# Rebuilding the stage ahead of the attention loop: block firsts and rows read from the input, counting on ScalarE, 64 degree classes, tables beside the last tiles

## The reference

```
xn  = layernorm(x)
q, k, v = xn @ Wq.T + bq, xn @ Wk.T + bk, xn @ Wv.T + bv      # 8 heads of 32
sim = sum(q[dst] * k[src]) / sqrt(32);  p = softmax over the edges of one dst
x   = x + (sum over edges of p * v[src]) @ Wo.T + bo  +  mix(xn)
x   = x + ffn(layernorm(x))       # 8 experts, top 1, capacity 977 per expert
```

## Time and profile before

| | us |
|---|---|
| median of 3 runs | 2949.57 |
| lowest and highest run | 2949.54, 2952.72 |
| span of the profiled execution, first to last instruction | 2949.1 |
| busy PE, DVE, ACT, POOL in that span | 2127.7, 2429.0, 1010.5, 2119.7 |

### The profile page before, as it was taken

The page is one execution under the profiler, slowest core; times in us unless marked ns, Lnnn a source line. Parts: engine busy times, 40 slices in busy tenths (PEclk is TensorE's granted clock), DMA queues, the critical chain, the costliest instruction groups (busy, mean ns, idle before and its releaser), DMA issues. The chain is left out here.

```text
span 2949.1 us, 36213 instructions
## 1 busy us (share of the span) xinstructions
PE 2127.7 (72%) x9400; PEld 1712.6 (58%) x9401; DVE 2429.0 (82%) x3296; ACT 1010.5 (34%) x4314; POOL 2119.7 (72%) x2220
## 2 busy tenths in 40 slices
PE   5675777767776777767888876556666655599998
PEld 4473555555565666555666554444444435599997
DVE  5676788888888999999999888899999985366665
ACT  3220555556566666611111111011111114345353
POOL 4465777777777777777777777777777775567785
PEclk9796888998999999989999898887888885599999
DMA  6746777777777777788888887777777758423331
GB/s 218 246 156 172 208 210 208 207 211 217 219 218 219 218 219 218 227 233 241 257 255 257 254 241 213 212 211 211 211 211 211 211 162 288 152 70 76 88 92 15
DMA packets 257830, 587.19 MB, mean 199 GB/s; under 512 B 49410, under 2 KB 135505, under 8 KB 257565
## 3 DMA queue, kind: packets, MB, share of 16 engines
q0 software_dynamic: 150480, 467.10, 57.4%
q1 hardware_dynamic: 97947, 109.47, 11.2%
q10 hardware_dynamic: 9296, 9.44, 0.9%
HBM read 519.05 MB, written 71.76 MB: 200 GB/s over the span
## 5 line engine op out<-in xcount | busy, mean ns | idle before, releaser
L1041 POOL DMA_INDIRECT wide<-kv_d,arena x1099 | 1051.0, 956 | 335.0 <-issue 326.7
L1340 PE MATMUL ps<-wide,arena 128*128 128x264 f32 x2432 | 694.6, 448 | 238.9 <-DVE wide L1444 238.6
L1340 PEld LDWEIGHTS ps<-wide,arena 128*128 128x128 f32 x2432 | 530.2, 223 | 395.2 <-DVE wide L1444 283.4
L1041 POOL DMA_INDIRECT arena<-kv_d,arena x539 | 515.3, 956 | 164.3 <-issue 159.1
L1176 ACT ACTIVATE ps<-wide 128x256 f32 x229 | 88.8, 388 | 1324.2 <-DVE arena L1410 1282.5
L1413 DVE TENSOR_REDUCE arena<-arena 128x64 f32<-128x2048 f32 x229 | 523.5, 2286 | 7.9
L1340 PE MATMUL ps<-arena 128*128 128x264 f32 x1216 | 350.4, 451 | 128.7 <-DVE arena L1444 128.7
L1410 DVE TENSOR_TENSOR arena<-wide,ps 128x2048 f32<-128x2048 f32 x153 | 349.3, 2283 | 105.7 <-DMA wide<-kv_d,arena 105.6
L1340 PEld LDWEIGHTS ps<-arena 128*128 128x128 f32 x1216 | 267.0, 225 | 209.0 <-DVE arena L1444 152.9
L1444 DVE TENSOR_TENSOR wide<-wide,ps 128x2112 f32<-128x2112 f32 x152 | 356.8, 2347 | 24.4 <-ACT arena L1191 24.4
L141 PE MATMUL ps<-halves 128*128 128x256 f32 (+2 forms) x2304 | 361.9, 319 | 3.2 <-DVE halves L1703 1.6
(11 more groups left out here) (310 smaller groups left out, 3137.8 us busy)
## 6 DMA issues: line engine op xcount, KB each, us to landing
wide<-kv_d,arena POOLq DMA_INDIRECT x1099, 3.8
arena<-in_w SPq DMA_DIRECT2D x16, 1024.0 KB, 5.4
kv_d<-wide SPq DMA_DIRECT2D x49, 260.0 KB, 2.2
arena<-xn_d SPq DMA_DIRECT2D x82, 128.0 KB, 3.4
arena<-kv_d,arena POOLq DMA_INDIRECT x539, 3.8
hb_d<-arena SPq DMA_DIRECT2D x16, 516.0 KB
q_d<-wide SPq DMA_DIRECT2D x49, 128.0 KB, 2.7
xn_d<-arena SPq DMA_DIRECT2D x7, 896.0 KB, 9.0
```

The source lines that it names most:

```text
L1041: e.indirect_dma_start(out=kvb[k][:, j, :], out_offset=None, in_=kv_d, in_offset=bass.IndirectOffsetOnAxis(ap=ixb[k][:, j:j + 1], axis=0)) ...
L1340: m = e.matmul(psE[(k + 1) % 3][:, 0:264], ident, kvb[b][:, j, 256:ROW], start=(j == 0), stop=(j == J - 1))
```

## The change

- **Firsts and rows from the input.** `dst` is no longer copied to DRAM and padded. SyncE's first three issues read each block's first edge from the input. The block numbers are made ahead of the first tile, as element offsets, capped at the last whole block, and the first three row gathers are issued there. The other 47 keep coming three per tile, each behind a tile's product; each quarter of them has a semaphore of its own.
- **Counting on ScalarE.** The comparison and sum over quarters on VectorE are replaced by 50 activations `Sign` with a sum, one per column, three per tile from tile 6 on; the list `LANDED` says from which tile on a quarter may be counted. `ranks` starts in tile 23 without waiting steps and with two steps per tile.
- **64 classes.** The degree one-hots, sums, prefixes and rank products use 64 classes instead of 128, eight columns per step instead of four, and VectorE multiplies and sums a step in two instructions.
- **Tables beside the last tiles.** `tables` no longer waits for the stores or issues queries; it runs on with the steps of the last tiles, and one of its products moves from `ps[6]` to `ps[4]`.
- **Queries.** The function `first_queries` follows the last tile: SyncE writes the edge numbers into `q_d` there, and GpSimd's 13 query gathers wait for that, for the sort and for the last stores.
- **Weights and biases.** Their order becomes keys, queries, values, so that the bias takes two instructions instead of three. ScalarE scales and rounds the weights in three pieces; group 0 is centred on ScalarE like the others.
- **Blanks.** A blank tile is written to DRAM once, and SyncE fills `hb_d` from it by two transfers in each of the loop's eight `AUX` rounds.

The core of the diff:

```diff
+CLS = 64
...
+LANDED = ((6, 13), (11, 26), (15, 39), (19, 50))
+SORTED_FROM = 23
...
+        t_f0 = v(V.memset(fi_i[:, 12:13], 1 << 20))
+        whole = 12 * 128 * 128
+        dma(Y, fi_i[:, 0:12], dst[0:whole].rearrange("(a p j) -> p a j", p=128, j=128)[:, :, 0], s_fi, allow_slow_non_contiguous=True)
+        wait(Y, t_f0)
+        rest_ = NB - 1 - 12 * 128
+        dma(Y, fi_i[0:rest_, 12:13], dst[whole:whole + rest_ * 128].rearrange("(p j) -> p j", j=128)[:, 0:1], s_fi, allow_slow_non_contiguous=True)
+        t_fi = dma(Y, fi_i[rest_:rest_ + 1, 12:13], dst[(NB - 1) * 128:(NB - 1) * 128 + 1].rearrange("(a j) -> a j", j=1), s_fi)
...
-        dma(Y, flat(dst_d)[0:E].rearrange("(a b) -> a b", b=825), dst.rearrange("(a b) -> a b", b=825), s_ed)
...
-        assert E + 86 == NB * 128
...
-        t_fi = dma(Y, fi_i, dst_d.rearrange("(a p) j -> p a j", p=128)[:, :, 0], s_fi, allow_slow_non_contiguous=True)
+        s_bl = sem("s_bl")
...
+        t_bl = dma(Y, blank_d, blank, s_bl)
 
...
+        t = v(V.tensor_scalar(out=off, in0=blk, scalar1=128.0, scalar2=float(E - 128), op0=ALU.mult, op1=ALU.min))
+        wait(V, t)
+        t_off = v(V.tensor_copy(blki, off))
...
-        def take_rows(t_blk):
-            wait(G, t_blk, t_ed)
-            for c in range(50):
-                s_row.inc(G.indirect_dma_start(out=rows[:, c, :], out_offset=None, in_=dst_d,
-                                               in_offset=bass.IndirectOffsetOnAxis(ap=blki[:, c:c + 1], axis=0)), 16)
...
+        def take_rows():
+            for q, (c0, c1) in enumerate(QUARTERS):
+                for c in range(c0, c1):
+                    s_row[q].inc(G.indirect_dma_start(out=rows[:, c, :], out_offset=None, in_=dst.rearrange("(a b) -> a b", b=825),
+                                                      in_offset=bass.IndirectOffsetOnAxis(ap=blki[:, c:c + 1], axis=1)), 16)
...
-            wait(Y, t_own)
-            ids_of = q_d.rearrange("(p c) d -> p c d", c=NT)
-            dma(Y, ids_of[:, 0:32, 256:QI], own[0].bitcast(f32), s_own)
-            t_own_.append(dma(Y, ids_of[:, 32:NT, 256:QI], own[1].bitcast(f32), s_own))
...
+        fetching.append(take_rows())
+        fetch_some(t_off)
...
+        def count_some(n):
+
+            for _ in range(n):
+                c = counted[0]
+                q = [i for i, (c0, c1) in enumerate(QUARTERS) if c0 <= c < c1][0]
+                wait(S, (s_row[q], s_row[q].n), t_half)
+                counted[1] = a(S.activation(less[:, c, :], rows[:, c, :], ACT.Sign, bias=nodeh[:, c:c + 1], scale=-1.0,
+                                            accum_out=fine[:, c:c + 1]))
+                counted[0] = c + 1
...
         def ranks():
...
-            fetching[0] = take_rows(v(V.tensor_copy(blki, blk)))
-            for _ in range(WAIT_ROWS):
-                yield
-            assert fetching[0] is None
-            wait(V, (s_row, s_row.n))
-            for c0, c1 in QUARTERS:
-                t = v(V.tensor_tensor(less[:, c0:c1, :], rows[:, c0:c1, :],
-                                      nodeid[:, c0:c1].unsqueeze(2).to_broadcast([128, c1 - c0, 128]), ALU.is_lt))
-                yield
...
-                t = v(V.tensor_reduce(fine[:, c0:c1], less[:, c0:c1, :], AX.X, ALU.add))
...
+            wait(V, counted[1])
+            t = v(V.scalar_tensor_tensor(out=rp, in0=fine, scalar=0.5, in1=half, op0=ALU.mult, op1=ALU.add))
...
+                t = v(V.tensor_tensor(OHc[:, c0:c1, :], iota[:, 0:CLS].unsqueeze(1).to_broadcast([128, c1 - c0, CLS]),
+                                      fine[:, c0:c1].unsqueeze(2).to_broadcast([128, c1 - c0, CLS]), ALU.is_equal))
...
-            for q in range(14):
-                if q < 13:
+            for q in range(8):
...
-                    for i in range(min(4, NT - 4 * q)):
-                        c = 4 * q + i
-                        T.matmul(b[:, i * 128:(i + 1) * 128], start_[:, c:c + 1].to_broadcast([128, 128]), ident, start=True, stop=False)
-                        m = T.matmul(b[:, i * 128:(i + 1) * 128], trib, OHc[:, c, :], start=False, stop=True)
+                    for i in range(min(8, NT - 8 * q)):
+                        c = 8 * q + i
+                        T.matmul(b[:, i * CLS:(i + 1) * CLS], start_[0:CLS, c:c + 1].to_broadcast([CLS, 128]), ident[0:CLS, 0:CLS],
+                                 start=True, stop=False)
+                        m = T.matmul(b[:, i * CLS:(i + 1) * CLS], trib, OHc[:, c, :], start=False, stop=True)
...
-                    for c in range(4 * u, min(4 * u + 4, NT)):
-                        i = c - 4 * u
-                        t = read[u] = v(V.scalar_tensor_tensor(out=of_rank[:, i, :], in0=ps[5 + 2 * (u % 2)][:, i * 128:(i + 1) * 128], scalar=1.0,
-                                                               in1=OHc[:, c, :], op0=ALU.mult, op1=ALU.mult, accum_out=rankf[:, c:c + 1]))
+                    t = read[u] = v(V.tensor_tensor(of_rank[:, 0:n, :], r3(ps[5 + 2 * (u % 2)][:, 0:n * CLS], CLS), OHc[:, 8 * u:8 * u + n, :], ALU.mult))
+                    wait(V, t)
+                    t = v(V.tensor_reduce(rankf[:, 8 * u:8 * u + n], of_rank[:, 0:n, :], AX.X, ALU.add))
                 yield
...
+            wait(Y, *t_own_)
+            ids_of = q_d.rearrange("(p c) d -> p c d", c=NT)
+            dma(Y, ids_of[:, 0:32, 256:QI], own[0].bitcast(f32), s_own)
+            t_ids = dma(Y, ids_of[:, 32:NT, 256:QI], own[1].bitcast(f32), s_own)
+            wait(G, *t_sorted, t_ids, *t_kv)
+            for c in range(FIRST_Q):
+                (s_q0 if c < RING else s_q).inc(G.indirect_dma_start(out=qi[:, c, :], out_offset=None, in_=q_d,
+                                                                     in_offset=bass.IndirectOffsetOnAxis(ap=permS[:, c:c + 1], axis=0)), 16)
...
             t_ds = v(V.tensor_copy(permS[:, 0:NT], fx))
-            while not t_kv:
-                yield
-            assert t_own_
-            wait(V, t_hz, *t_own_, *t_kv)
...
-            wait(G, t_q49, t_ds, *t_own_, *t_kv)
-            for c in range(FIRST_Q):
-                (s_q0 if c < RING else s_q).inc(G.indirect_dma_start(out=qi[:, c, :], out_offset=None, in_=q_d,
-                                                                     in_offset=bass.IndirectOffsetOnAxis(ap=permS[:, c:c + 1], axis=0)), 16)
+            t_sorted.append(t_ds)
+            t_sorted.append(v(V.memset(qi[:, NT, :], 0.0)))
+            wait(V, t_bl, t_src)
...
+                made_.append(sp.inc(T.matmul(ps[(5, 4, 7)[i]][0:1, 0:CH], cf[:, i:i + 1], ind[0:50, :], start=True, stop=True)))
...
-            wait(V, t_hz)
...
+        a(S.activation(wh[:, :, 256:512], W[:, :, 256:512], ACT.Copy, scale=SC))
+        a(S.activation(wh[:, :, 0:256], W[:, :, 0:256], ACT.Copy))
+        t_wh = a(S.activation(wh[:, :, 512:768], W[:, :, 512:768], ACT.Copy))
...
+        wait(V, t_x[0])
+        spread(xbuf[0], range(7))
+        wait(V, root(7))
+        t_nm[0] = minus_mean()
+        for i in range(2):
+            t_n[0, i] = center_s(xbuf[0], i, t_nm[0])
...
+        wait(V, t_wh)
+        v(V.scalar_tensor_tensor(out=wl[:, :, 256:512], in0=W[:, :, 256:512], scalar=SC, in1=wh[:, :, 256:512].bitcast(f32),
+                                 op0=ALU.mult, op1=ALU.subtract))
+        v(V.tensor_tensor(wl[:, :, 0:256], W[:, :, 0:256], wh[:, :, 0:256].bitcast(f32), ALU.subtract))
+        t_W = v(V.tensor_tensor(wl[:, :, 512:768], W[:, :, 512:768], wh[:, :, 512:768].bitcast(f32), ALU.subtract))
...
-                if grp > 0 and j + 2 < 7:
+                if j + 2 < 7:
...
-                if t > WAIT_ROWS:
-                    pump()
+                landed = max([c for u_, c in LANDED if t >= u_], default=0)
+                count_some(min(3, landed - counted[0]))
+                if t == SORTED_FROM:
+                    assert counted[0] == 50
+                    more[0] = ranks()
+                pump()
...
-                    v(V.tensor_tensor(stage[u % 3][:, 0:256], b0[:, 0:256], bal[:, 0:256], ALU.add))
-                    v(V.tensor_tensor(stv[u % 3][:, :, 0:32], r3(b0[:, 256:512], 32), r3(bal[:, 256:512], 32), ALU.add))
-                    t_bias[u] = v(V.tensor_tensor(stage[u % 3][:, 520:776], b1_[:, 0:256], bal[:, 512:768], ALU.add))
+                    v(V.tensor_tensor(both[u % 3], r3(b0[:, :], 256), r3(bal[:, 0:512], 256), ALU.add))
+                    t_bias[u] = v(V.tensor_tensor(stv[u % 3][:, :, 0:32], r3(b1_[:, 0:256], 32), r3(bal[:, 512:768], 32), ALU.add))
...
-                    if 16 <= u < 32:
-                        i = u - 16
-                        wait(Y, t_em)
-                        t_hz = dma(Y, hb_d[i * 512:(i + 1) * 512, :].rearrange("(p j) d -> p (j d)", p=128), empty, s_hz)
-                    if u == 0:
-                        more[0] = ranks()
...
+        while len(t_sorted) < 2:
+            pump()
+        first_queries()
...
+            def blanks():
```

(40 more changed lines are left out.)

125 lines of the change are left out of this document (54 added, 71 removed).

## The result

The changed kernel takes **2983.78 us** (median of four runs, 2980.28 to 2987.88) against 2949.56: a ratio of 1.0111, 95% interval 1.0099 to 1.0123, so 34 us slower where 18 us faster was forecast. Its profiled run took 2986.06 us, with a span of 2984.8.

A forecast was written before the change was run, and what follows sets the result against it. GpSimd's loop, 1.26 us per gather, was taken as the bound, so its start counts: -4.6 + 4 (start), -20.1 (sort, tables), +8.5 (edge numbers), -6.1 (queries), 18.2 us earlier: 2931.4 us, range 2923 to 2943.

The forecast's parts named there:

- the rank column: TensorE's cost per column while ranks are made: 0.25 us taken, so 25 us in four tiles (bounds 21 and 29).
- Tables: Table and mask work moved into tiles 41 to 46: 27.5 us for those six tiles, where bare tiles take 13.5.
- Rival D: Round trips in the 12 table steps cost 6 us more, edge numbers land after 16: 2940.5 us; chance 0.10.
- halved one-hots: In the sort with 64 classes, four one-hots of about 1.8 us halve and lose 3.5 us.
- The rest of the sort: Nine tiles after the ranks: 46.9 us less a 2.56 us wait for a store of q, so 44.3.
- rival B: ScalarE's Signs stand wholly on the tiles' path, 50 x s instead of 4 us; 2969 us at 0.83; chance 0.05.
- the waits for rows: Delay of the Signs in the early tiles by rows landing after tile 19 is due: 1 us.
- The edge numbers' loss: Transfers to q_d behind the last tile's stores land 13 us after the last bias begins: loss 8.5 us.
- the thirteen queries without a gap: GpSimd's 13 query gathers ahead of the loop run at 1.26 us each, 16.3 us if nothing interrupts them.
- rival C: Blanks of hb_d in the loop's rounds slow it: 2963 us if half their DMA time delays it; chance 0.05.
- the wait for the index loads: After the thirteen queries, 1 to 2 us for SyncE's six index loads; queries and wait take 17.9 us.
- Rival A: The query stalls ahead of the loop have another cause than the mask and stay: 2935.5 us; chance 0.12.

The follow-up runs named there:

- e14: Changed kernel with each step's eight 64-row fp32 products grouped ahead of its eight 128-row bf16 ones: 2958.7 us.
- e9: As e8, but the tables stay beside tiles 41 to 46 and only the mask stands behind the last tile: 2938.5 us.
- e6: Changed kernel with the work on the tables, mask included, started only when the last tile is done: 2967.3 us.
- e8: Changed kernel with the edits of e4, e5 and e6 together: 2922.6 us.
- e4: Changed kernel with each start split into a bf16 value and remainder, stacked on 128 rows for one bf16 product: 2953.4 us.
- e5: Changed kernel with the two edge-number transfers issued as soon as the last edge number is gathered: 2977.7 us.
- e1: Changed kernel with 128 classes again and four columns per step: 2949.4 us.
- e3: Changed kernel with four columns per step instead of eight, 64 classes and 64-row products kept: 2968.7 us.
- e12: Changed kernel with 128 classes, four columns per step, early edge numbers and tables behind the last tile: 2925.2 us.
- e13: As e8, with all row gathers issued at once and the mask made in five pieces beside the last tiles: 2914.4 us.

## Why the prediction was wrong

By its own stations, forecast against measured, in us after the start. The forecast counted from the first of the three bias additions of a tile, the measured bias times are the second of two, 0.6 us after the first:

| station | forecast | measured | step, forecast | step, measured |
|---|---|---|---|---|
| first one-hot | 99.5 | 99.54 | | |
| bias 26 | 120 | 122.40 | | |
| bias 30 (ranks) | 145 | 175.85 | 25 | 53.45 |
| bias 39 (rest of the sort) | 189.3 | 223.88 | 44.3 | 48.03 |
| bias 45 (tables) | 216.8 | 261.27 | 27.5 | 37.39 |
| bias 48 | 223.5 | 276.19 | 6.7 | 14.92 |
| first query | 236.5 | 290.11 | 13 | 13.92 |
| first loop gather | 254.4 | 309.60 | 17.9 | 19.49 |

**The step that failed is the rank column**: "With 64 output columns a column costs between half (0.16) and all of 0.33; I take 0.25". It measured 0.49 to 0.79, outside the bounds, and 28.4 of the 55.2 us between the forecast and the measured first loop gather are there. Both bounds were taken from a row of a 128-row product among 128-row products. The diff also halved the rows of one product of each pair. No row of before showed such a pair, so the upper bound of 0.33 had nothing under it. The 28.4 are two things: with 0.49 for all 49 columns, the step would be 4 x 3.2 + 49 x 0.49 = 36.8 us (an estimate), 11.8 above the forecast, and the other 16.6 came with the granted clock of 0.58, of which the forecast said nothing. With most of the changes of rows taken away (e14) the stretch took 25.42 us and the column 0.27, so the rest of the step, tiles and count, was sized rightly. No rival had it.

**Tables** were the second: 27.5 forecast, 37.39 measured, and 8.2 more in the three tiles that the forecast had called bare, since the mask fell there (e9: 7.5 us of it). The forecast added VectorE's time to the tiles' and no waiting. But the steps need TensorE between them, which runs in order. In the tile of the small products VectorE first makes a 2.28 us mean of weights that has nothing to do with the tables; TensorE waits 5.16 us for the chain behind it, and then runs the next tile's products at the lower clock (0.78 us for 512 columns at 245.47, where one takes 0.48 at 251.92). VectorE's timeline, then TensorE's:

```profile
237.86 2.28 DVE L718 TENSOR_REDUCE arena<-wide 128x32 f32<-128x2048 f32 x1
...
241.47 0.52 DVE L627 SCALAR_TENSOR_TENSOR arena<-arena 50x300 f32<-50x300 f32 x1
```

```profile
242.04 3.16 PE L631 MATMUL ps<-arena 50*1 50x300 f32 x6 [5.16 <-DVE arena L627]
...
245.47 0.78 PE L142 MATMUL ps<-rear_halves,row_halves 128*128 128x512 f32 x1
```

From bias 42 to bias 43 that is 250.30 - 237.53 = 12.8 us for one tile. Rival D named these round trips but gave them 6 us. Tables and mask behind the last tile, where they were, make the tiles after bias 39 shorter by 28.7 us (e6 against the changed kernel) or 25.2 (e8 against e4), and give back 6.7 (e6) or 2.4 (e8 against e5) between the last bias and the first loop gather.

**Smaller misses.** Up to bias 26 the forecast took off 3.5 us for halved one-hots. VectorE's one-hots did halve (1.03 instead of 1.89 us), but bias 26 comes no earlier for it: 122.40 with 64 classes, 122.10 with 128 (e1). The rest of the sort was put at 44.3 and took 48.03; it took 47.7 to 48.9 also where ranks were quick (e4, e8, e14), and 44.3 and 45.4 where it lay three tiles later (e3, e12).

**Right**: the first row gather at 14.22 (14), the first product at 20.75 (21.2), the Signs at 0.39 us from one to the next (0.35). The first one-hot came at 99.54 (99.5), so the Signs do not stand wholly on the path and rival B is out, but that the number is so close is luck: the waits for rows were put at 1 us and are 5.73 and 8.21, and the forecast had left in two waits of the tiles of before, 4.56 and 4.44 us for stores of q, which are gone. The edge numbers' loss (on the same mark, the tile's last bias addition, 13.92 less 3.79 is 10.1, against 8.5), the thirteen queries without a gap and the unchanged loop (rival C out) came as forecast; the wait for the index loads was 3.45 us instead of 1 to 2.

**Rival A**, by which the long query gathers have nothing to do with the mask, falls too: with the mask ahead of them there is no gap, with the mask beside them gathers of 6.17 and 2.62 us are back (e8), in e6 the long one comes well before the index loads begin, and with pieces it is gone while the index loads stay (e13). The Trainium skill, on SBUF — State Buffer, Who interferes with whom, infers that a plain two-input operation does not hold up descriptor writing. As a guide to these gathers that fails: the one of 6.17 us began 0.9 us ahead of a two-input operation of 3.67 us and ended after it, and in e13 one took 2.11 us instead of 0.95 with a two-input subtraction and a memset of 0.06 us beside it. Which part of a gather is held up, the rows don't show.

What stays open: why the granted clock falls while TensorE's rows show it busy all the time. Over the ranks it was 0.52 to 0.66 in each of the five kernels that alternate 64 and 128 rows column by column, and 0.88 to 1.00 in the others; e14 has the same products, grouped, and 1.00. So the alternation brings the fall with it, but the runs don't show by what.

## What to carry to other kernels

When a product gets smaller, look at what stands next to it on TensorE: a 64-row product between 128-row ones costs more than the full one, and filling up with zeros, grouping by shape, or stacking two halves into 128 rows brings the time back. Work that goes back and forth between two engines, each of which runs in order, was cheapest where the path waits for something else; count its round trips, not only its busy time. And follow a moved transfer to its new place in the queue: here the same two transfers cost 10 us behind the last tile (13.9 less 3.9 from last bias to first query).

## What the runs showed of the hardware

A pair of a 64-row fp32 and a 128-row bf16 product, 64 columns each, took 0.49 us at 2.4 GHz and 0.79 at 1.2 GHz alternating, 0.27 at 2.4 GHz when grouped by eight. With zeros up to 128 rows it took 0.28 and 0.53 at the two clocks, and two bf16 products of 128 rows 0.06 at 2.4 GHz. TensorE, by its rows busy 17.00 of 17 us, was granted 0.50 of its clock. A gather that GpSimd issues in 0.95 us took 5.93 (e6) and 6.17 (e8) across VectorE's mask work of 3.67 and 1.10 us, and 2.11 (e13) to 2.62 (e8) across a two-input subtraction of 2.3 us.
